# Two dense feed-forward stages: where TensorE turns the attention outputs, and in which unit VectorE and ScalarE take the norms, the low halves and the row sums

## The reference

```
m0..m5 = split(silu(c) @ ada_w + ada_b, 6)
y = modulate(layer_norm(x), m0, m1);  x = x + m2 * attention(y)
y = modulate(layer_norm(x), m3, m4)
x = x + m5 * (gelu(y @ w1 + b1) @ w2 + b2)      # w1: 288 x 1152, w2: 1152 x 288
```

## Time and profile before

| | us |
|---|---|
| median of 3 runs | 1524.46 |
| lowest and highest of them | 1519.86, 1529.19 |
| the profiled execution, its own time | 1524.85 |
| its span | 1523.1 |

### The profile page before, as it was taken

How to read it: one execution, slowest core, us unless ns; L and a number is a source line. 1 busy time by engine, 2 the same in 40 slices (tenths; PEclk the granted TensorE clock), 3 DMA queues, 4 the chain that set the end, 5 groups by cost and what they waited for, 6 DMA issues and landing times.

```text
span 1523.1 us, 26994 instructions
## 1 busy us (share of the span) xinstructions
PE 1414.7 (93%) x8989; PEld 968.4 (64%) x8989; DVE 1215.1 (80%) x2569; ACT 927.6 (61%) x1675; POOL 731.6 (48%) x1651
## 2 busy tenths in 40 slices
PE   6899999988999999996899999899999999989998
PEld 5653334767899888875543334789876333478886
DVE  7779996886998667776889997677967999876564
ACT  4449997455666545764369987434734899764432
POOL 0556650113665517126656566676765666663000
PEclk9989999999999999998999999999999999999999
DMA  7765530028664544535654521201056454110001
GB/s 212 209 189 123 149 97 3 29 89 238 186 153 133 159 121 114 146 115 172 193 147 141 136 58 5 49 5 21 5 181 186 118 145 108 15 6 1 1 1 63
DMA packets 109053, 160.72 MB, mean 106 GB/s; under 512 B 34666, under 2 KB 76636, under 8 KB 108782
## 3 DMA queue, kind: packets, MB, share of 16 engines
q1 hardware_dynamic: 101778, 142.84, 30.9%
q0 software_dynamic: 7136, 16.15, 8.4%
HBM read 114.74 MB, written 39.58 MB: 101 GB/s over the span
## 4 chain that ended last, share of the span: by engine, by line
PE 44%; DVE 24%; ACT 4%; issue 3%; DMA 3%; SPq 1%; another core or an unknown queue 1%; POOL 1%; DVEq 0%; ACTq 0%; POOLq 0%
PE psum L1664 18%; DVE minus_max L2705 8%; PE psum L2150 6%; PE psum L2295 6%; PE psum L1854 4%; PE psum L1843 3%; PE psum L1817 3%; DVE minus_max L2700 2%; PE psum L1727 1%; DMA raw_a<-in_L_cond_b 1%; PE psum L1998 1%; DVE x_norm L2543 1%; ACT x_mod L1450 1%; DVE qk_parts L2588 1%
## 5 line engine op out<-in xcount | busy, mean ns | idle before, releaser
L1583 ACT ACTIVATE probs<-psum 128x512 f32<-128x512 f32 x768 | 403.3, 600 | 70.6 <-PE psum L1843 63.6
L2705 DVE TENSOR_REDUCE minus_max<-psum 128x1 fp32r<-128x512 f32 x606 | 376.8, 681 | 41.0 <-PE psum L1817 40.0
L1817 PE MATMUL psum<-k_stack,q_stack 54*128 54x512 f32 x768 | 258.8, 464 | 11.8 <-DVE minus_max L2705 5.0
L1664 PE MATMUL psum<-x_split,w_hi 128*128 128x512 f32 (+1 forms) x684 | 243.1, 398 | 6.7 <-issue 2.4
L1843 PE MATMUL psum<-q_stack,k_stack 55*128 55x512 f32 x768 | 241.1, 447 | 8.4 <-ACT probs L1583 8.3
L1843 PEld LDWEIGHTS psum<-q_stack,k_stack 55*128 55x128 f32 x768 | 117.3, 188 | 163.0 <-ACT probs L1583 154.3
L1854 PE MATMUL psum<-probs,o_t 128*19 128x512 f32 x1536 | 205.9, 608 | 6.1 <-ACT o_t L1562 3.2
L1100 POOL TENSOR_TENSOR qr_m<-qr_m 64x8 f32<-64x8 f32 (+35 forms) x544 | 186.3, 342 | 42.6
L1817 PEld LDWEIGHTS psum<-k_stack,q_stack 54*128 54x128 f32 x768 | 113.4, 189 | 96.4 <-DVE minus_max L2705 72.4
L1095 POOL TENSOR_TENSOR qr_m<-qr_rows 64x288 f32<-64x288 f32 (+31 forms) x64 | 45.3, 707 | 255.4 <-DMA qr_rows<-qr_rows 255.4
L1664 PEld LDWEIGHTS psum<-x_split,w_hi 128*128 128x128 f32 x684 | 129.5, 191 | 30.6 <-issue 7.6
(11 more groups left out here) (453 smaller groups left out, 3213.9 us busy)
## 6 DMA issues: line engine op xcount, KB each, us to landing
qk_parts_d<-qk_parts SPq DMA_DIRECT2D x48, 512.0 KB
raw_b<-in_L_cond_w SPq DMA_DIRECT2D x36, 432.0 KB
q_stack<-qk_parts_d SPq DMA_DIRECT2D x96, 144.0 KB
k_stack<-qk_parts_d SPq DMA_DIRECT2D x96, 144.0 KB
raw_a<-in_L_cond_w SPq DMA_DIRECT2D x36, 384.0 KB
q_stack<-qk_parts_d SPq DMA_DIRECT2D x96, 72.0 KB
k_stack<-qk_parts_d SPq DMA_DIRECT2D x96, 72.0 KB
moe_out_d<-branch SPq DMA_DIRECT2D x9, 576.0 KB, 3.5
```

The costliest lines, as they stand in the source:

```text
L1583: act.activation(PE_[:, v // 4, 2 * hf + pr, :], psum[:, score_bank(16 * i + v), :], ACT.Exp, scale=SCALE).then_inc(s_e, 1)
L1664: i = pe.matmul(dst, a, r, start=(n == 0), stop=(n == len(terms) - 1))
L1817: return pe.matmul(psum[:, bank, :], Q6[half(hf, STK), g, pr, P * qt:P * qt + P], K6[half(hf, STK), g, pr, :], start=True, stop=True)
L2705: dve.tensor_reduce(MX[:, i % 2, col:col + 1], psum[:, bank, :], AX.X, ALU.max, negate=True).then_inc(s_mx, 1)
```

## The change

No instruction of TensorE, ScalarE or GpSimd is added or removed; only their places in the order change, and VectorE has the same work too. The core of the diff:

```
-NEXT_UNIT = (25, 27, 32)
+NEXT_UNIT = (25, 28, 32)
 QKV_UNIT = (30, 32, 33)
-P_UNIT = 31
+P_UNIT = 26
+STATS_UNIT = (20, 30)
+QKV_LOW_UNIT = (32, 33, 34)
+FIRST_ORDER = (("1", 0), ("1", 1), ("2", 0), ("1", 2), ("2", 1), ("2", 2))
...
-                    at_ = HM * b - O_STEPS + k + (k == 8)
+                    at_ = HM * b - O_STEPS + k + (k in (0, 8))
...
# ScalarE
                     if j == 0:
                         o_t(l, B * HG - 1)
-                        split_hi_first(l, "1", 2)
-                    if j <= 2:
-                        split_hi_first(l, "2", j)
+                        split_hi_first(l, "2", 0)
                     for b, k in steps_beside(j):
...
+                    if j == 1:
+                        split_hi_first(l, "1", 2)
+                    if j in (2, 3):
+                        split_hi_first(l, "2", j - 1)
# TensorE
                     for b, k in steps_beside(j):
-                        if k == 8:
+                        if k == 8 or (k == 0 and b >= 2):
                             to_ffn(l, b, k)
                     if j >= 2:
                         second(f0 + (j - 2) // UNITS, (j - 2) % UNITS)
...
                     for b, k in steps_beside(j):
-                        if k != 8:
+                        if k != 8 and not (k == 0 and b >= 2):
                             to_ffn(l, b, k)
# VectorE
-                if f == sets_of(l)[-1] and l + 1 < LAYERS and b in (0, 2):
-                    stats(b)
...
+                    for b, k in steps_beside(j):
+                        if (b, k) == (1, 7) or (k == 0 and b >= 2):
+                            to_ffn(l, b, k)
                     hidden_parts(f, u)
...
+                    if l + 1 < LAYERS and j == J - UNITS + STATS_UNIT[0]:
+                        stats(0)
+                    if l + 1 < LAYERS and j == J - UNITS + STATS_UNIT[1]:
+                        moments(2)
+                    if l + 1 < LAYERS and j == J - UNITS + STATS_UNIT[1] + 1:
+                        rsqrt(2)
                     for b, k in steps_beside(j):
-                        if k < 2:
+                        if k == 1 or (b, k) == (1, 0):
                             to_ffn(l, b, k)
                     if j == 0:
+                        split_lo_first(l, "2", 0)
+                    if j in (3, 4):
+                        split_lo_first(l, "2", j - 2)
+                    for b, k in steps_beside(j):
+                        if k >= 2 and (b, k) != (1, 7):
+                            to_ffn(l, b, k)
+                    if j == 2:
                         split_lo_first(l, "1", 2)
-                    if j <= 2:
-                        split_lo_first(l, "2", j)
-                    for b, k in steps_beside(j):
-                        if k >= 2:
-                            to_ffn(l, b, k)
-                    if j == HM // 2 and l + 1 < LAYERS:
+                    if j == HM and l + 1 < LAYERS:
                         mod_cols(l + 1)
-                    if l + 1 < LAYERS and j >= J - UNITS and u - 1 in QKV_UNIT:
-                        split_lo_qkv(l + 1, QKV_UNIT.index(u - 1))
+                    if l + 1 < LAYERS and j >= J - UNITS and u in QKV_LOW_UNIT:
+                        split_lo_qkv(l + 1, QKV_LOW_UNIT.index(u))
```

More of the change, by code:

```diff
@@ L634, in build @@
             else:
-                events += [(kind, first_set(l), i) for kind in ("1", "2") for i in range(3)]
+                events += [(kind, first_set(l), i) for kind, i in FIRST_ORDER]
             if l == 0:
@@ L640, in build @@
             elif l + 1 < LAYERS:
-                events += [("q", l + 1, i) for i in range(KC + 1)] + [("p", l + 1)]
-                events += [("q", l + 1, i) for i in range(KC + 1, 3 * (KC + 1))]
+                events += [("p", l + 1)] + [("q", l + 1, i) for i in range(3 * (KC + 1))]
         split_no = {k: i for i, k in enumerate(events)}
```

## The result

| | before | changed |
|---|---|---|
| median, us (6 runs of each) | 1520.23 | 1506.95 |
| lowest and highest | 1518.33, 1529.19 | 1504.47, 1509.54 |
| span of the profiled execution | 1523.1 | 1503.2 |

The ratio of the times is 0.9908, with a 95% interval of 0.9886 to 0.9929: 14 us faster (11 to 17). Two later timings, on other chips, gave 0.9914 each (0.9883 to 0.9945, 0.9889 to 0.9939). Two later executions in a slow state (2025 us in run e9, 1892 us of the kernel before beside it, at a granted clock of 0.60 and 0.65) are left out of the ratios. The three further runs of the kernel before brought its median from 1524.46 to 1520.23, so of the 6.35 us between the forecast of 1513.3 and the 1506.95, 4.2 lie in the median that I started from; the change itself was forecast at 11.1 and gave 13 to 14.

The account below looks back on a forecast made before the run. TensorE, busy in 93% of the span, was taken as the bound, so only its waits and slow clock could give time. Stage 1 -6.0 and stage 2 -5.1 make -11.1: 1513.3 us, range 1506 to 1520.

Parts of the forecast that it names:

- head, stage 1: Units 0 to 3: fewer weight pieces ahead on VectorE, so the turn no longer waits for o_lo; -1.9 us.
- head, stage 2: The same start of stage 2, where the wait for o_lo was 1.06; -1.1 us.
- group 1 to 2: Units 5 to 9: norm earlier -0.65, turn waits +0.2, turn_o behind the up product -0.55; -1.0 us in each stage.
- group 2 to 3: Units 16 to 18: up product covers turn_o's wait -1.5, clock kept -1.8, new wait +0.3; -3.0 us in each stage.
- moved sums: Unit 20 of stage 1: stats(0)'s 4.2 us ahead of group 3's first attn_add delay the projection; +0.4 us, from 0 to 1.5.
- the end of stage 1: From unit 22 VectorE has no idle time, so only what it gains in its holes arrives; -0.5 us, -1.5 to +0.5.
- The norm: Group 1's norm ahead of hid_lo of unit 5: -0.65 us a stage, though the held gelu leaves x_mod only some 0.2.
- row 977.40: x_mod of group 1 on ScalarE in stage 1, behind the gelu of unit 7, which was in time there.
- My own sign of being wrong: Unit 7: the forecast is wrong if late hid_lo(5) makes its gelu wait over 1 us.
- Unit 21's wait: Stage 1: a new wait under 1 us for attn_add was to show there.
- The wait at the turn in unit 34: End of stage 1: the turn of the next layer's norm was to wait more than now.
- Rival C: Slower: stats(0) makes VectorE late by 4.2 us at unit 20, later seams late with dropped clock; some +1.5, 1526; chance 0.05.

Follow-up runs that it names:

- e9: The changed kernel with the old order of the weight pieces at the head of a dense stage; ratio 0.9952 to the kernel before.
- e4: The kernel before with only the second half of stage 1 changed (moved sums, weight halves, third layer's first norm of group 1); ratio 1.0004.
- e2: The kernel before with only turn_o of groups 2 and 3 (first pair) behind the up product, its o_rows moved on VectorE; ratio 0.9977.
- e10: The changed kernel with group 1's norm back, moments(0) and rsqrt(0) in units 18 and 19, the projection's low half in unit 22; ratio 0.9878.
- e12: The changed kernel with group 1's norm behind the low half again and the projection's low half in unit 22 instead of 26; ratio 0.9891.
- e1: The kernel before with only the new order of the weight pieces at the head of a dense stage; ratio 0.9966.
- e7: The changed kernel with group 1's norm back behind the low half of unit 5; ratio 0.9928 to the kernel before.
- e3: The kernel before with only group 1's norm ahead of the low half of unit 5; ratio 1.0016.
- e6: The changed kernel, unchanged, timed and profiled again; ratio 0.9914 to the kernel before, stages 298.11 us.
- e15: The changed kernel, unchanged, timed and profiled once more; ratio 0.9914 to the kernel before, stages 298.45 us.
- e11: The changed kernel with only moments(0) at the end of unit 18 and rsqrt(0) at the end of unit 19; ratio 0.9921.
- e8: The changed kernel with stats(0), stats(2), weight halves and the third layer's norm of group 1 back in their old places; ratio 0.9915.
- e16: The same kernel as e10, timed again beside the changed kernel; ratio 0.9904 to the kernel before.
- e5: The kernel before, unchanged, profiled a second time; the two stages took 312.35 us.
- e13: The kernel before, unchanged, profiled a third time; the two stages took 308.85 us.
- e14: The kernel before, unchanged, profiled a fourth time; the two stages took 312.90 us.

## Why it came out so, step by step

Means of four profiles before and three after, gelu to gelu, against the terms of the forecast:

| term | forecast | measured |
|---|---|---|
| head, stage 1 (units 0 to 4) | -1.9 | 19.39 to 17.25: -2.1 |
| head, stage 2 | -1.1 | 19.77 to 17.41: -2.4 |
| group 1 to 2, stage 1 (4 to 9) | -1.0 | 24.24 to 22.84: -1.4 |
| the same, stage 2 | -1.0 | 23.46 to 23.13: -0.3 |
| group 2 to 3, stage 1 (16 to 18) | -3.0 | 14.85 to 10.28: -4.6 |
| the same, stage 2 | -3.0 | 12.81 to 10.21: -2.6 |
| moved sums, stage 1 (18 to 23) | +0.4 | 21.16 to 21.79: +0.6 |
| the end of stage 1 (23 to 35) | -0.5 | 50.12 to 50.45: +0.3 |
| sum | -11.1 | -12.4 |

**Group 2 to 3 in stage 1 is the step that failed, in its reason and in its size.** I gave 1.5 to the cover of the up product, 1.8 to the clock and nothing to the removal of `stats(0)`. The runs say: `stats(0)` away alone (e4), 11.61 instead of 14.85, -3.2; `turn_o` behind the up product alone (e2), 15.81, no gain; both, 10.09 to 10.66 (11.21 in e10 and e12). The clock was worth nothing there, since e1 at full clock took 13.35 and the first profile at 0.87 took 13.43, with VectorE busy for all but 0.9 us of both. The bound was VectorE's queue from `ffn_add` to `x_tail`, with `stats(0)` in it. A wait that a slower TensorE has filled leaves no bracket on TensorE, but VectorE's row 1026.12, in the profile that I had, ends 0.06 ahead of the up product. I took the 1.81 between the two seams as "mostly the lower clock" without following VectorE to its last row. In stage 2, without sums to make, the reason was right: 1.55 for the cover (11.63 to 10.08) and 1.6 for the clock, but the latter only in three of four executions.

**Head, stage 2.** Too small by 1.3: in the first profile this head took 18.15, in the other three 19.95 to 20.56, with waits for `o_lo` of 1.16, 1.82 and 1.91 where the earlier trace rows have 1.06, and of 1.00, 0.74 and 0.26 at the first down product, where I had counted none. The mechanism was right, as e1 and e9 show, and the size was that of a lucky execution.

**The norm.** Of row 977.40 I had said that it "neither shows nor excludes" that the held gelu holds `x_mod`: e7 and e3 show it. My own sign of being wrong came too: in the three profiles of the changed kernel gelu of unit 7 comes 7.17 to 8.45 after that of unit 5, against 6.43 to 6.66 before, 1.0 us or more late in five of six places. The Trainium skill ("Perfetto Trace Analysis", Tensor Engine Instruction) has ScalarE and VectorE take their work strictly in order, and the rows of e6 and e7 above agree, with `x_mod` 1.26 later. But I let the norm still gain. Six profiles with this move and the seam's (changed, e6, e15, e11, e8, e9) take 22.88 on the mean for units 4 to 9 of stage 2, four without it (e7, e12, e10, e16) 22.21; in stage 1 it is 22.62 against 22.11. The move costs some 0.5 to 0.7 a stage. What the seam gained there came from `turn_o` alone (e2: 22.05 in stage 2).

**Sums and the end.** Unit 21's wait was 0.36 where 0.4 was forecast. The wait at the turn in unit 34 was there, 2.72; the end of the stage got no shorter. Rival C did not come: VectorE's holes took the sums, and the granted clock from unit 29 to 35 stayed at 1.00 in two of the three profiles of the changed kernel. It can fall there: it was 0.93 to 0.95 in e15, e7, e9, e11, e12 and e16, and 0.94 in the first profile before and in e1, where the sums had not moved.

**Between the stages** 1.5 us remain of means of 240.9 and 239.4. The variants ranged from 238.98 to 243.03 with no tie to a part, so I don't count it to the change. Three of the four longest (243.59, 243.03, 241.92) are those with the slow clock behind `k_stack`. Ahead of stage 1, where the order is the same, the means differ by another 6.6 (first gelu at 940.5 and 933.9). Together the profiles give -20.5, more than the timed 13 to 14: the four profiled executions of the kernel before lie 5.0 above the medians of their chips on the mean, the three of the changed kernel 1.4 below. So the profiles place the gain, and its size is that of the times; whether some of the stages' -12.4 is chance too stays open.

That the parts need each other is shown for `stats(0)` and the seam by e2, e4 and e8. For the whole it stays open: by the times the four ratios multiply to 0.9963, against 0.991, each known to some 0.002, but by the stages of one profile each the parts give 19.7 alone, against 12.4 together.

## What to carry to other kernels

Look for the second-last wait before a stretch is priced: what would stop the engine had it arrived on time? Here VectorE's queue, with `stats(0)` in it, held the stretch and the slow clock stood in front of it. Comparing the stretch with each engine's busy time in it shows such a bound where no bracket does. Where a sum of small terms is made, one profile is not enough: the same kernel's two stages varied by 5.9 us over four executions, half of what the change gave. And an instruction moved ahead of a small one on an engine that others wait for has to be followed to the third engine: the 0.3 to 0.5 that TensorE's turn gained were taken back by ScalarE, whose `x_mod` fell 1.2 further behind it.

## What the runs showed of the hardware

A wait of 1.75 to 1.93 us ahead of `turn_o` of group 3 stands in 14 places, with the same rows around it. In four of them (1020, 1407, 1416, 1424) the granted clock over the next 5 us was 0.66, the lower level of 1.2 GHz in most of it, and in ten (as at 1410) 1.00. In the 22 places where `turn_o` stands behind the up product and waits 0.31 or less it was 1.00. In stage 2 the clock was lowered in three of four profiles of the kernel before, and in none of e1, e3 and e4.

VectorE's multiply in `ffn_add` (four of 128x288) took 3.09 us in stage 1 in e5 and e13 and 2.40 in e14, with GpSimd at work, and 1.55 where GpSimd has nothing to do, as in stage 2 of e5. In stage 1 of the first profile it took 1.56, while GpSimd waited for a DMA until 1017.08. So it depends on what GpSimd does in those us. Timeline of e5, GpSimd beside the 3.09 us, and VectorE's row in stage 2, then the first profile:

```profile
1004.09 0.67 POOL L1095 TENSOR_TENSOR qr_m<-qr_rows 64x250 f32<-64x250 f32 x1 [3.46 <-DMA qr_rows<-qr_rows]
1004.72 0.81 POOL L1096 TENSOR_TENSOR qr_m<-qr_rows 64x250 f32<-64x250 f32 x1
...
1401.35 1.55 DVE L3325 TENSOR_TENSOR branch<-branch,gate_mlp 128x288 f32<-128x288 f32 x4
```

```profile
1015.51 1.56 DVE L3325 TENSOR_TENSOR branch<-branch,gate_mlp 128x288 f32<-128x288 f32 x4
...
1017.08 0.62 POOL L1095 TENSOR_TENSOR qr_m<-qr_rows 64x249 f32<-64x249 f32 x1 [3.36 <-DMA qr_rows<-qr_rows]
```

The Trainium skill ("SBUF — State Buffer", SBUF: two separate sides) has an operation of VectorE with two SBUF inputs and one of GpSimd that reads SBUF exclude each other for a whole instruction. The rows agree: the 3.09 are 1.54 more than the 1.55, and GpSimd's two rows beside them take 0.67 and 0.81. I had said that the sum would be the same by it. From one execution to the next it was not, since GpSimd's work falls on other instructions: this multiply stands ahead of `stats(0)`, and its 1.53 more in e5 are about the 1.40 between 13.43 and 14.83 for units 16 to 18. Of the 16.29 in e14 it explains less (2.40, 0.84 more).
